# One column of a Householder step, yc, computed on VectorE behind rt instead of on GpSimd

## Chip, cores and metric

One core of a Trainium2 chip runs the whole program. Its engines are TensorE (PE, with its weight loads as PEld), VectorE (DVE), ScalarE (ACT), GpSimd (POOL) and SyncE (SP, which issues the DMAs). The metric is the device time of one execution in microseconds (us); durations of single instructions are given in ns or us.

## What is computed

The reference is a chain of four residual blocks on x of shape 128 x 64 x 128: a spectral graph layer, a mixture of eight experts, a graph layer with LSTM windows, and a second mixture of experts. Only the first block matters here, since it needs the eigenvectors of a 64 x 64 matrix:

```python
deg = jnp.sum(A, axis=0) + jnp.sum(A, axis=1) - jnp.diagonal(A)
d_inv_sqrt = jnp.where(deg > 0, jax.lax.rsqrt(deg), 0.0)
L = jnp.diag(deg) - A
L_norm = d_inv_sqrt[:, None] * L * d_inv_sqrt[None, :]
_, U = jnp.linalg.eigh(L_norm)
agg = jnp.einsum('mn,bnd->bmd', U.T, features)
h = jax.nn.relu(agg @ W1 + b1)
out = h @ W2 + b2
return jnp.einsum('nm,bmd->bnd', U, out)
```

The kernel finds U itself: it brings the matrix to tridiagonal form with 62 Householder steps, finds eigenvalues by counting sign changes, and the vectors by recurrences. The change lies in the Householder steps.

## The kernel before

The function `spectrum` writes one instruction stream for each engine (the blocks `@block.gpsimd`, `@block.scalar`, `@block.tensor`, `@block.vector`). There is no scheduler: each engine runs its stream in the order written, and the streams meet only at semaphores (`then_inc` and `wait_ge`). The 62 steps are unrolled; in step i the active columns are i+1 to 63, so the tiles shrink from 63 columns to 2. The matrix M (64 x 128) holds in its left half what is left to be reduced, and in its right half the accumulated reflections.

What one step does, with the names and lines that matter:

- The row x (on all 128 partitions, so that every lane has the whole row) has just been written by VectorE (L536). ScalarE takes its squared length s2 (L291) and the root nrm (L293). VectorE makes rnrm (L523), t (L526) and rt = 1/t (L527), the factor that normalizes the Householder vector.
- GpSimd takes the sign nsg of the leading element (L227), scales the column form xc of the row to xsc (L230) and the row to xs (L231). When rt is there it makes the column yc = xsc * rt - e (L234), then CB (L235), which keeps the off-diagonal element for later, and, when ntau is there, ntyc = yc * ntau (L238).
- TensorE makes two products with M in each step: with xsc (L384, into bank 1), which waits for M of the step before and for xsc, and with yc (L386, into bank 2). Each is a 4-byte product and shows as two matrix multiplications.
- VectorE makes the row form y of the vector (L530) behind rt, and ntau (L532). ScalarE makes q from the first product (L297) and ny = y * ntau (L299). VectorE takes the dot product h2 of y and q (L115, two instructions), and with ny, h2 and q it writes the next row x (L536).
- VectorE then updates M twice. The first update (L540) needs the second product and ntyc. Between the two stand the dot product that takes xc out of the new row (L115 with h_junk_x and h_xc) and the dot product mc. The second update (L546) writes the M that the next step's first product waits for.

So yc has two forms of use: as the weights of the second product, and as an input of ntyc. Both meet again in the first update of M, L540.

Of the kernel before, what the change touches and what calls it, by code (L numbers as in the profile page):

```python
# [8 lines left out]
ALU = mybir.AluOpType  # L9
# [5 lines left out]
N = 64  # L15
# [97 lines left out]
def dot(dve, junk, a, b, out):  # L113

    return dve.tensor_tensor_reduce(out=junk, in0=a, in1=b, scale=1.0, scalar=0.0, op0=ALU.mult, op1=ALU.add,  # L115
                                    accum_out=out)


def spectrum(nc, k, sem, A, loads, x_tok):
# [5 lines left out]
    with ExitStack() as own:  # L125
        def sb(name, shape, dtype=F32):
            return own.enter_context(nc.sbuf_tensor("h_" + name, shape, dtype))

        def col(name, rows=P):
            return sb(name, [rows, 1])[:, :]  # L130
        pivot, minus = sb("pivot", [P, P]), sb("minus", [P, N])
# [6 lines left out]
        s2, nrm, rnrm, t, rt, sg, nsg, ntau, xc, h2, nudge = (  # L138
            col(n) for n in "s2 nrm rnrm t rt sg nsg ntau xc h2 nudge".split())
        scratch = sb("scratch", [P, 2 * GT, D])  # L140
        xsc, yc, ntyc, mc = (col(n, N) for n in "xsc yc ntyc mc".split())
# [41 lines left out]
        @block.sync  # L183
        def _(sp):
            for h in range(2):
                sp.dma_start(A[:, h * N:(h + 1) * N], loads["adj"]).then_inc(s_adj, 16)
            for q in range(4):
                r = slice(q * TILES // 4, (q + 1) * TILES // 4)
                sp.dma_start(k.X[:, r, :], x_tok[:, r, :]).then_inc(s_x[q], 16)
            for dst, src in loads["rows"](rows, rows2):  # L190
                sp.dma_start(dst, src).then_inc(s_rows, 16)
            for dst, src in loads["raw"](raw):
                sp.dma_start(dst, src).then_inc(s_raw, 16)
            sp.wait_ge(s_const, CONSTS)
            for dst, src in loads["rest"]:
                sp.dma_start(dst, src).then_inc(s_load, 16)
            sp.wait_ge(s_load, 16 * len(loads["rest"]))

        @block.gpsimd
        def _(pool):  # L200
            pool.memset(ident[:, :], 0.0).then_inc(s_pool, 1)
            pool.memset(pivot[:, :], 0.0).then_inc(s_pool, 1)
            pool.wait_ge(s_pool, 2)
            pool.affine_select(out=ident[:, :], in_=ident[:, :], compare_op=ALU.not_equal, fill=1.0, base=0,
                               pattern=[[-1, P]], channel_multiplier=1).then_inc(s_pool, 1)
            consts = [pool.memset(ones[:, :], 1.0), pool.memset(BDU[:, :], 0.0), pool.memset(BDUT[:, :], 0.0), pool.memset(BDAT[:, :], 0.0),
                      pool.memset(k.upper[:, :], -1.0), pool.memset(k.w_gate1[:, :, :], 0.0)]
            consts += [pool.memset(k.prio[:, e:e + 1], float(E - e)) for e in range(E)]
            consts += [pool.iota(dst, pattern=[pattern], base=base, channel_multiplier=lanes,
                                 allow_small_or_imprecise_dtypes=True) for dst, pattern, lanes, base in  # L210
                       ((order, [0, 1], 1, 0), (k.irow[:, :], [1, IROW], 0, 0), (k.token[:, :], [P, TILES], 1, 1))]
            for ins in consts:
                ins.then_inc(s_const, 1)
            pool.memset(pivot[:, N:N + 1], 1.0).then_inc(s_const, 1)

            pool.wait_ge(s_const, CONSTS - 1)
            pool.affine_select(out=k.upper[:, :], in_=k.upper[:, :], compare_op=ALU.is_ge, fill=0.0, base=0,
                               pattern=[[-1, P]], channel_multiplier=1).then_inc(s_const, 1)
            for i in range(STEPS):
                if i == ROWS_AT:  # L220
                    pool.wait_ge(s_rows, 16 * 5)
                    pool.tensor_tensor(rows[0:SKIPS * GATES, :], rows[0:SKIPS * GATES, :], rows2[:, :],
                                       ALU.add).then_inc(s_sum, 1)
                pool.wait_ge(s_row, i + 1)
                if i:
                    pool.wait_ge(s_beta, i)
                pool.tensor_scalar(nsg, x[:, i + 1:i + 2], 0.0, -0.5, ALU.is_lt, ALU.add).then_inc(s_sign, 1)  # L227
                pool.wait_ge(s_sign, i + 1)
                pool.wait_ge(s_xcol, i + 1)
                pool.tensor_scalar(xsc, xc[0:N, :], nsg[0:N, :], 4.0, ALU.mult, ALU.mult).then_inc(s_xs, 1)  # L230
                pool.tensor_scalar(xs[:, i + 1:N], x[:, i + 1:N], nsg, 4.0, ALU.mult, ALU.mult).then_inc(s_xs, 1)  # L231
                pool.wait_ge(s_inverse, 2 * i + 1)
                pool.wait_ge(s_xs, 2 * i + 1)
                pool.tensor_scalar(yc, xsc, rt[0:N, :], minus[0:N, i + 1:i + 2], ALU.mult, ALU.add).then_inc(s_ycol, 1)  # L234
                pool.tensor_scalar(CB[:, i:i + 1], t, nsg, None, ALU.mult).then_inc(s_beta, 1)  # L235
                pool.wait_ge(s_ycol, i + 1)
                pool.wait_ge(s_inverse, 2 * i + 2)
                pool.tensor_scalar(ntyc, yc, ntau[0:N, :], None, ALU.mult).then_inc(s_ntyc, 1)  # L238

            def normalized(g, tiles):  # L240
                if g >= 2:
                    pool.wait_ge(s_tokens, g - 1)
                for j in range(tiles):
                    n = g * GT + j
                    last = pool.tensor_scalar(k.ZB[g % 2][:, j * P:(j + 1) * P], k.X[:, n, :], k.mean[:, n:n + 1],
                                              k.rstd[:, n:n + 1], ALU.subtract, ALU.mult)
                last.then_inc(s_z, 1)

            for turn in range(PASSES):
                for c in range(len(LEAVES) - 1):  # L250
                    if turn and c < len(LEAVES) - 2:
                        if turn == 1 and c == 0:
                            pool.wait_ge(s_scale, 2)
                        normalized((turn - 1) * (len(LEAVES) - 2) + c, GT)
            pool.wait_ge(s_scale, 4)
            for g in range(EARLY, GROUPS):
                normalized(g, GT // 2)
# [214 lines left out]
        def _(dve):  # L472
            link = Chain(dve, ch)
            tt_, ts_, stt = dve.tensor_tensor, dve.tensor_scalar, dve.scalar_tensor_tensor
# [43 lines left out]
            def reflect(i):  # L518

                r, rest, at = slice(i + 1, N), slice(i + 2, N), slice(i + 1, i + 2)  # L520

                dve.wait_ge(s_rooted, i + 2)
                link(dve.reciprocal(rnrm, nrm))  # L523
                if i:
                    dve.wait_ge(s_beta, i)
                link(stt(out=t, in0=rnrm, scalar=s2, in1=nrm, op0=ALU.mult, op1=ALU.add))  # L526
                dve.reciprocal(rt, t).then_inc(s_inverse, 1)  # L527
                dve.wait_ge(s_inverse, 2 * i + 1)
                dve.wait_ge(s_xs, 2 * i + 2)
                link(stt(out=y[:, r], in0=xs[:, r], scalar=rt, in1=pivot[:, N:2 * N - 1 - i],  # L530
                         op0=ALU.mult, op1=ALU.subtract))
                dve.reciprocal(ntau, y[:, at]).then_inc(s_inverse, 1)  # L532
                dve.wait_ge(s_q, i + 1)
                link(dot(dve, junk_h[:, r], y[:, r], q[:, r], h2))
                dve.wait_ge(s_scaled, i + 1)
                stt(out=x[:, rest], in0=ny[:, rest], scalar=h2, in1=q[:, rest],  # L536
                    op0=ALU.mult, op1=ALU.add).then_inc(s_row, 1)
                dve.wait_ge(s_ym, i + 1)
                dve.wait_ge(s_ntyc, i + 1)
                got_M = link.put(stt(out=M[:, i + 1:P], in0=ps[2][0:N, i + 1:P], scalar=ntyc, in1=M[:, i + 1:P],  # L540
                                     op0=ALU.mult, op1=ALU.add))
                dve.wait_ge(s_row, i + 2)
                dot(dve, junk_x[:, rest], x[:, rest], ident[:, rest], xc).then_inc(s_xcol, 1)
                link.need(got_M)
                link(dot(dve, junk_m[0:N, r], M[:, r], y[0:N, r], mc))
                stt(out=M[:, r], in0=ny[0:N, r], scalar=mc, in1=M[:, r], op0=ALU.mult, op1=ALU.add).then_inc(s_matrix, 1)  # L546

            for i in range(STEPS):
                reflect(i)
# [1945 lines left out]
```

## Time and profile before

| what | value |
|---|---|
| median of 3 runs | 1427.07 us (1426.35 to 1429.05) |
| profiled execution, its time | 1429.24 us |
| profiled execution, its span from the first to the last instruction | 1427.5 us |
| granted TensorE clock over the span | 0.902 of full speed |
| PE, PEld busy | 1110.5 us (78%), 823.2 us (58%) |
| DVE, ACT, POOL busy | 813.1 us (57%), 747.9 us (52%), 537.7 us (38%) |

The page of the profile cuts the span into 40 slices. The Householder steps fill the first four and most of the fifth, about 11 to 173 us. The shares of the whole span say little of them: there each step is a chain over four engines, and what counts is which instruction starts late in it and why. That is read from the timeline of single steps, where each row gives start, duration, engine, line and what the engine had waited for.

### The profile page before, as it was taken

The page shows a single profiled execution, that of the slowest core. Times are in us where ns is not written, and L with a number is a line of the kernel's source. Part 1 is how long each engine was busy: PE and PEld are TensorE (multiplying, and loading weights), DVE is VectorE, ACT ScalarE, POOL GpSimd, SP SyncE. Part 2 cuts the span into 40 slices and gives each one's busy share as a digit, 9 for nine tenths or more (in the row PEclk, how much of TensorE's full clock was granted, in tenths as well). Part 3 has the DMA queues.
Part 4 walks back from the last instruction along what each step waited for, and adds up shares of the span by engine and source line. Part 5 has one row for each costly group of instructions (what it writes and reads, how often), then busy time and mean ns, then how long its engine had stood idle before and what let it go on. Part 6 is the DMA issues. An engine that isn't in the chain of part 4 may idle for free. (4 is left out here: it accounts for less than half of the span.)

```text
span 1427.5 us, 27849 instructions
## 1 busy us (share of the span) xinstructions
PE 1110.5 (78%) x6302; PEld 823.2 (58%) x6303; DVE 813.1 (57%) x3799; ACT 747.9 (52%) x2079; POOL 537.7 (38%) x837
## 2 busy tenths in 40 slices
PE   3444424568744999999949999999999689929995
PEld 2223313456644999999936663445444245529995
DVE  7777798958772433354558973444444478622221
ACT  4555555515322666666626765655555366415552
POOL 5666513302577770255447500000000005645554
PEclk9999965879757999999969999999999799959998
DMA  9500000000112332333311100000000002243330
GB/s 260 144 1 1 1 1 1 1 4 16 36 64 85 118 120 66 89 103 104 102 46 50 40 1 0 0 1 0 0 1 0 4 6 85 90 130 110 106 103 27
DMA packets 85701, 75.57 MB, mean 53 GB/s; under 512 B 13207, under 2 KB 74848, under 8 KB 85613
## 3 DMA queue, kind: packets, MB, share of 16 engines
q1 hardware_dynamic: 71788, 44.64, 11.3%
q0 software_dynamic: 13824, 29.98, 6.7%
q8 instruction: 28, 0.46, 0.1%
q14 instruction: 61, 0.49, 0.1%
HBM read 41.72 MB, written 33.37 MB: 53 GB/s over the span
## 5 line engine op out<-in xcount | busy, mean ns | idle before, releaser
L1249 POOL DMA_INDIRECT z<-spent,seats x64 | 63.3, 990 | 393.5 <-DVE spent L1370 376.1
L1716 ACT ACTIVATE c_H<-ps,c_b 128x128 f32<-128x128 f32 x576 | 156.9, 383 | 99.5 <-PE ps L1762 99.5
L2278 PE MATMUL ps<-BIG,spent 128*128 x364 | 156.1, 578 | 3.3 <-ACTq L2291 3.3
L1762 PE MATMUL ps<-ZS,c_w 128*128 128x128 f32 x1152 | 142.5, 277 | 2.9 <-ACT ZS L1705 1.7
L1748 PE MATMUL ps<-spent,c_H 128*128 x1152 | 140.3, 275 | 0.0
L1762 PEld LDWEIGHTS ps<-ZS,c_w 128*128 128x128 f32 x1152 | 136.0, 194 | 3.9 <-ACT ZS L1705 2.4
L1748 PEld LDWEIGHTS ps<-spent,c_H 128*128 128x128 f32 x1152 | 134.3, 192 | 0.0
L2278 PEld LDWEIGHTS ps<-BIG,spent 128*128 128x128 f32 x364 | 69.7, 192 | 84.7 <-issue 84.7
L2286 PE MATMUL ps<-e_hs,spent 128*128 128x512 f32 (+1 forms) x256 | 110.0, 572 | 0.0
L897 POOL DMA_INDIRECT z<-BIG,spots x64 | 63.5, 993 | 111.1 <-DVE spots L1014 93.7
L1616 POOL DMA_INDIRECT c_rows<-y,seats x64 | 60.6, 946 | 113.9 <-DMA y<-c_ys 60.0
L1861 POOL DMA_INDIRECT out_dram<-X,BIG x72 | 70.5, 979 | 78.5 <-DVE X L1878 65.5
L1642 DVE COPY c_w<-spent 128x512 f32 x144 | 56.2, 433 | 75.1 <-PE ps L1762 71.0
L1897 ACT ACTIVATE j_H<-ps,bias_cols 128x256 f32<-128x256 f32 x144 | 60.4, 471 | 64.5 <-PE ps L1934 63.7
L384 PE MATMUL ps<-h_M,h_xsc 64*128 64x63 f32 (+61 forms) x124 | 37.5, 392 | 70.7 <-POOL h_xsc L230 68.5
L1661 DVE TENSOR_TENSOR c_ys<-ps,b_dn 128x128 f32<-128x128 f32 x144 | 35.2, 286 | 98.3 <-PE ps L1748 97.4
L1874 DVE TENSOR_TENSOR X<-ps,b_dn 128x128 f32<-128x128 f32 x72 | 17.6, 286 | 120.0 <-PE ps L1922 120.0
L384 PEld LDWEIGHTS ps<-h_M,h_xsc 64*128 64x128 f32 x124 | 31.0, 309 | 87.3 <-DVE h_M L546 85.9
L2286 PEld LDWEIGHTS ps<-e_hs,spent 128*128 128x128 f32 x256 | 48.6, 190 | 56.1 <-issue 53.2
L2005 POOL DMA_INDIRECT d_Y<-y,seats x64 | 63.5, 993 | 40.7 <-SPq L1989 19.4
L1621 POOL DMA_INDIRECT z<-BIG,spots x64 | 64.3, 1005 | 19.5 <-issue 19.5
L1934 PE MATMUL ps<-ZS,w_up 128*128 128x256 f32 x288 | 69.7, 386 | 1.5 <-ACT ZS L1886 1.5
(534 smaller groups left out, 2599.2 us busy)
## 6 DMA issues: line engine op xcount, KB each, us to landing
BIG<-z SPq DMA_DIRECT2D x72, 129.0 KB, 2.1
ZB<-z SPq DMA_DIRECT2D x144, 64.0 KB
y<-c_ys SPq DMA_DIRECT2D x72, 128.0 KB
spent<-in_L_ffn_W_dram SPq DMA_DIRECT2D x1, 2048.0 KB
spent<-in_L_ffn_W_dram SPq DMA_DIRECT2D x8, 256.0 KB
w_dn<-in_L_ffn_Wd_dram SPq DMA_DIRECT2D x8, 256.0 KB
z<-BIG,spots POOLq DMA_INDIRECT x128, 2.2
z<-j_padding SPq DMA_DIRECT2D x9, 129.0 KB, 2.6
```

What stands on the lines that cost most here:

```text
L384: pe.matmul(ps[1][:, r], xsc.to_broadcast([N, P]), M[:, r], start=True, stop=True).then_inc(s_xm, 1)
L897: pool.indirect_dma_start(z, bass.IndirectOffsetOnAxis(ap=k.spots[:, n, 0:1], axis=0), z_of(n), None, bounds_check=E * STRIDE - 1, oob_is_ ...
L1249: pool.indirect_dma_start(z, bass.IndirectOffsetOnAxis(ap=k.seats[:, 0, n:n + 1], axis=0), k.R[:, row(n), :], None, bounds_check=E * STRID ...
L1621: pool.indirect_dma_start(z, bass.IndirectOffsetOnAxis(ap=k.spots[:, n, 1:2], axis=0), k.BIG[:, n * P:(n + 1) * P], None, bounds_check=2 * ...
L1716: act.activation(H[u][:, c, h * P:(h + 1) * P], UP[u][c // 2][:, o:o + P], ACT.Gelu, bias=b1[u][h][:, c:c + 1]).then_inc(gelu, 1)
L1748: last = pe.matmul(Y[u][:, h * D:(h + 1) * D], H[u][:, c, h * P:(h + 1) * P], w2[:, ds(es[h] * (C * D) + c * D, D)], start=(c == 0), stop= ...
L1762: pe.matmul(UP[u][c // 2][:, o:o + P], w1[u][h][:, c * P:(c + 1) * P], ZT[u][:, h * P:(h + 1) * P], start=True, stop=True).then_inc(up, 1)
L1861: pool.indirect_dma_start(out, bass.IndirectOffsetOnAxis(ap=Z[b][h][:, ROW - 1:ROW].bitcast(I32), axis=0), ys[b][h][:, :], None, bounds_ch ...
L1934: pe.matmul(UP[u][c // 2][:, c % 2 * SLOT_TILE:(c % 2 + 1) * SLOT_TILE], k.w_up1[:, c * P:(c + 1) * P], ZT[u][:, :], start=True, stop=True ...
L2005: pool.indirect_dma_start(Y[b][:, :], None, y, bass.IndirectOffsetOnAxis(ap=k.seat[1][:, n:n + 1], axis=0)).then_inc(fetched[b], 16)
L2278: last = pe.matmul(view(k.ps[4 * u + j], wide, lanes), k.w_ihT[:, w, :], state(i, u, s, p, wide, lanes), start=True, stop=(s == 0))
L2286: pe.matmul(view(k.ps[4 * u + j], wide, lanes), k.w_hhT[:, w, :], view(hs[u], wide, lanes), start=False, stop=True).then_inc(fed, 1)
```

## The change

In each of the 62 steps the instruction that makes yc leaves the stream of GpSimd and enters that of VectorE, between rt and y. Its wait for xsc goes with it. In steps after the first VectorE also waits for the ntyc of the step before, which still reads the old yc. GpSimd's next instruction, CB, keeps the wait for rt; ntyc waits for yc by a semaphore as before.

```diff
                 pool.wait_ge(s_inverse, 2 * i + 1)
-                pool.wait_ge(s_xs, 2 * i + 1)
-                pool.tensor_scalar(yc, xsc, rt[0:N, :], minus[0:N, i + 1:i + 2], ALU.mult, ALU.add).then_inc(s_ycol, 1)
                 pool.tensor_scalar(CB[:, i:i + 1], t, nsg, None, ALU.mult).then_inc(s_beta, 1)
                 pool.wait_ge(s_ycol, i + 1)
...
                 dve.reciprocal(rt, t).then_inc(s_inverse, 1)
                 dve.wait_ge(s_inverse, 2 * i + 1)
+                dve.wait_ge(s_xs, 2 * i + 1)
+                if i:
+                    dve.wait_ge(s_ntyc, i)
+                ts_(yc, xsc, rt[0:N, :], minus[0:N, i + 1:i + 2], ALU.mult, ALU.add).then_inc(s_ycol, 1)
                 dve.wait_ge(s_xs, 2 * i + 2)
                 link(stt(out=y[:, r], in0=xs[:, r], scalar=rt, in1=pivot[:, N:2 * N - 1 - i],
```

VectorE in one step before, from t to the dot product h2 (lines as in the kernel before):

```order
L526 SCALAR_TENSOR_TENSOR h_t<-h_rnrm,h_s,h_nrm 128x1 [waits h_beta,ch]
L527 RECIPROCAL h_rt<-h_t 128x1 [waits ch]
L530 SCALAR_TENSOR_TENSOR h_y<-h_xs,h_rt,h_pivot 128x62 [waits h_xs,h_inverse]
L532 RECIPROCAL h_ntau<-h_y 128x1 [waits ch]
L115 ISA h_junk_h,h_h<-h_y,h_q 128x62 [waits h_q]
```

The same place after the change, where the line numbers below the edit are larger by two:

```order
L524 SCALAR_TENSOR_TENSOR h_t<-h_rnrm,h_s,h_nrm 128x1 [waits h_beta,ch]
L525 RECIPROCAL h_rt<-h_t 128x1 [waits ch]
L530 TENSOR_SCALAR h_yc<-h_xsc,h_rt,h_minus 64x1 [waits h_ntyc,h_xs,h_inverse]
L532 SCALAR_TENSOR_TENSOR h_y<-h_xs,h_rt,h_pivot 128x62 [waits h_xs]
L534 RECIPROCAL h_ntau<-h_y 128x1 [waits ch]
L115 ISA h_junk_h,h_h<-h_y,h_q 128x62 [waits h_q]
```

One instruction more stands between rt and y, and so ahead of ntau and everything behind it; the wait for rt (h_inverse) is now yc's.

GpSimd in one step before:

```order
L227 TENSOR_SCALAR h_nsg<-h_x 128x1 [waits h_beta,h_row]
L230 TENSOR_SCALAR h_xsc<-h_xc,h_nsg 64x1 [waits h_xcol,h_sign]
L231 TENSOR_SCALAR h_xs<-h_x,h_nsg 128x62
L234 TENSOR_SCALAR h_yc<-h_xsc,h_rt,h_minus 64x1 [waits h_xs,h_inverse]
L235 TENSOR_SCALAR h_CB<-h_t,h_nsg 128x1
L238 TENSOR_SCALAR h_ntyc<-h_yc,h_ntau 64x1 [waits h_inverse,h_ycol]
```

GpSimd in the same step after:

```order
L227 TENSOR_SCALAR h_nsg<-h_x 128x1 [waits h_beta,h_row]
L230 TENSOR_SCALAR h_xsc<-h_xc,h_nsg 64x1 [waits h_xcol,h_sign]
L231 TENSOR_SCALAR h_xs<-h_x,h_nsg 128x62
L233 TENSOR_SCALAR h_CB<-h_t,h_nsg 128x1 [waits h_inverse]
L236 TENSOR_SCALAR h_ntyc<-h_yc,h_ntau 64x1 [waits h_inverse,h_ycol]
```

CB moves up to the place of yc, and ntyc stands right behind it, with the same two waits as before.

## Rows read from the trace of the kernel before

**Rows 1.** Windows, all Householder steps: stretch, length, then busy time by engine.

```profile
11.00:173.60 162.60, 73.45 (x248) 48.56 (x248) 127.69 (x872) 90.10 (x434) 109.99 (x373) 1.00 0.28 77
```

**Rows 2.** Timeline, a step of 35 columns: start, duration, engine, line, operands, [idle before].

```profile
88.04 0.26 DVE L536 SCALAR_TENSOR_TENSOR h_x<-h_ny,h_h,h_q 128x35 f32<-128x35 f32 x1
...
88.80 0.29 POOL L230 TENSOR_SCALAR h_xsc<-h_xc,h_nsg 64x1 f32<-64x1 f32 x1 [0.18 <-DVE h_xc L115]
...
89.23 0.61 PE L384 MATMUL ps<-h_M,h_xsc 64*128 64x35 f32 x2 [1.12 <-POOL h_xsc L230]
89.40 0.17 DVE L527 RECIPROCAL h_rt<-h_t 128x1 f32<-128x1 f32 x1
89.60 0.25 DVE L530 SCALAR_TENSOR_TENSOR h_y<-h_xs,h_rt,h_pivot 128x35 f32<-128x35 f32 x1
89.67 0.40 POOL L234 TENSOR_SCALAR h_yc<-h_xsc,h_rt,h_minus 64x1 f32<-64x1 f32 x1 [0.19 <-DVE h_rt L527]
89.89 0.16 DVE L532 RECIPROCAL h_ntau<-h_y 128x1 f32<-128x1 f32 x1
89.94 0.38 ACT L297 ACTIVATE h_q<-ps,h_nudge,h_rt 128x35 f32<-128x35 f32 x1 [0.76 <-PE ps L384]
...
90.12 0.59 PE L386 MATMUL ps<-h_M,h_yc 64*64 64x99 f32 x2 [0.28 <-POOL h_yc L234]
90.22 0.31 ACT L299 ACTIVATE h_ny<-h_y,h_ntau 128x35 f32<-128x35 f32 x1
...
90.35 0.20 DVE L115 CUSTOM_DVE_ANT_0 h_junk_h<-h_y,h_q 128x35 f32<-128x35 f32 x1 [0.30 <-ACT h_q L297]
...
90.63 0.25 DVE L536 SCALAR_TENSOR_TENSOR h_x<-h_ny,h_h,h_q 128x34 f32<-128x34 f32 x1
90.80 0.31 DVE L540 SCALAR_TENSOR_TENSOR h_M<-ps,h_ntyc,h_M 64x99 f32<-64x99 f32 x1
```

**Rows 3.** Timeline, a step of 12 columns that started late on VectorE.

```profile
147.99 0.16 DVE L532 RECIPROCAL h_ntau<-h_y 128x1 f32<-128x1 f32 x1
...
148.19 0.30 ACT L299 ACTIVATE h_ny<-h_y,h_ntau 128x12 f32<-128x12 f32 x1
...
148.59 0.23 DVE L536 SCALAR_TENSOR_TENSOR h_x<-h_ny,h_h,h_q 128x11 f32<-128x11 f32 x1 [0.22 <-ACT h_ny L299]
```

**Rows 4.** Timeline, an early step of 53 columns: ntau and ny.

```profile
40.84 0.16 DVE L532 RECIPROCAL h_ntau<-h_y 128x1 f32<-128x1 f32 x1
...
41.20 0.33 ACT L299 ACTIVATE h_ny<-h_y,h_ntau 128x53 f32<-128x53 f32 x1
```

**Rows 5.** Timeline, a late step of 3 columns.

```profile
169.70 0.16 DVE L532 RECIPROCAL h_ntau<-h_y 128x1 f32<-128x1 f32 x1
...
169.98 0.28 ACT L299 ACTIVATE h_ny<-h_y,h_ntau 128x3 f32<-128x3 f32 x1
...
170.13 0.30 POOL L238 TENSOR_SCALAR h_ntyc<-h_yc,h_ntau 64x1 f32<-64x1 f32 x1
...
170.36 0.22 DVE L536 SCALAR_TENSOR_TENSOR h_x<-h_ny,h_h,h_q 128x2 f32<-128x2 f32 x1
170.53 0.28 DVE L540 SCALAR_TENSOR_TENSOR h_M<-ps,h_ntyc,h_M 64x67 f32<-64x67 f32 x1
```

**Rows 6.** Timeline, VectorE behind the steps: two scalars from memory, then one.

```profile
177.72 0.31 DVE L572 TENSOR_SCALAR h_trial<-irow,h_nwidth,h_nlo 128x64 f32<-128x64 f32 x1
178.07 0.25 DVE L573 TENSOR_SCALAR BIG<-h_trial,h_diag 128x64 f32<-128x64 f32 x1
```

**Rows 7.** Timeline, VectorE: four equal instructions in a row, and two small ones.

```profile
1132.15 1.11 DVE L1315 TENSOR_SCALAR spent<-spent,mean,rstd 128x128 f32<-128x128 f32 x4
1133.18 0.68 DVE L1271 TENSOR_TENSOR spent<-X,ps 128x512 f32<-128x512 f32 x1
...
166.25 0.22 DVE L546 SCALAR_TENSOR_TENSOR h_M<-h_ny,h_mc,h_M 64x5 f32<-64x5 f32 x1
...
166.40 0.16 DVE L523 RECIPROCAL h_rnrm<-h_nrm 128x1 f32<-128x1 f32 x1
```

## The prediction

> **What bounds the kernel now.** I read the windows first, to see how long the Householder steps last: about 162 us, in which VectorE, the busiest engine, is busy 128 us, 79%, so no engine is full and the steps are a chain [rows 1]. 62 steps in 162 us are 2.6 us each. VectorE works on without a pause behind the steps (the next stage begins from the finished M), so a step that is longer by some time moves the end by that time.
>
> Then I read one step's timeline, from one x to the next, to see which instruction starts late and on whose account [rows 2]. x starts at 88.04 and again at 90.63: 2.59 us. In between lies this cycle. x lets the first update of M start, behind it xc, then xsc on GpSimd (88.80 to 89.09), then the first product (89.23 to 89.84), then q on ScalarE (89.94), ny behind it (90.22 to 90.53), and x again at 90.63. The reader is to see two things there. First, yc on GpSimd (89.67 to 90.07) and the second product (90.12 to 90.71) are not in that cycle: they go to the first update of M at 90.80, which starts 0.17 us behind x on the same engine. Second, there is a side branch on VectorE: rt ends at 89.57, y ends at 89.85, ntau at 90.05, and ny needs ntau. It starts at 90.22, since ScalarE is busy with q. So ntau has slack, but not much.
>
> How much is told by a step in which VectorE ran late [rows 3]. There ntau ended at 148.15 and ny started at 148.19: 0.04 us is the least that lies between them. ny ended at 148.49 and x started at 148.59; the row itself puts x's 0.22 us of idle time down to ny. The same 0.10 us lies between the end of ny and x in the undisturbed steps (90.53 to 90.63 [rows 2], 170.26 to 170.36 [rows 5]). So I read x as released by ny in every step, and every delay of ny as a delay of x.
>
> **The slack of ntau.** It is the gap from the end of ntau to the start of ny, less 0.04 us. With 53 columns: 41.00 to 41.20, slack 0.16 [rows 4]. With 35: 90.05 to 90.22, slack 0.13 [rows 2]. With 3: 169.86 to 169.98, slack 0.08 [rows 5]. It shrinks because y, q and ny shrink by different amounts. I take these three for the first 20, the next 20 and the last 22 steps.
>
> **The change part by part.**
>
> *yc enters VectorE ahead of y.* y then starts later by the start-to-start distance of yc and y, which I call the shift. The trace has no VectorE instruction of one column with two scalars read from memory (rt and the column of minus), so it is bounded by rows. Four instructions of that kind with 128 columns plus the start of the next take 1133.18 - 1132.15 = 1.03 us, 0.257 each [rows 7]; that is an upper end, since yc has one column. A lower end is a small instruction with one such scalar: the second update of M with 5 columns starts at 166.25, and the next instruction at 166.40, 0.15 us later although it lasts 0.22 [rows 7]. Between the two stand two estimates. With 64 columns, an instruction with two scalars takes 0.31 us where one with a single scalar takes 0.25 [rows 6]; the second scalar costs 0.06, which added to 0.15 gives 0.21. And 127 columns taken off the 0.257 at 0.7 ns each (x is 0.03 us longer with 34 columns than with 2, about 1 ns each [rows 2, 5], and here one tensor less is read) leave 0.17. I take 0.19, their middle. The duration of yc itself comes to 0.22 + 0.06 = 0.28 us.
>
> The Trainium skill (VectorE: DVE Perf Modes, The TRN2 errata) prices a VectorE instruction from and to SBUF at 58 cycles plus its columns, which for one column at its 0.96 GHz is an estimate of 0.06 us; by that the shift would lie under the slack of every step and the sum would be nothing. The trace doesn't agree: 0.15 us is the distance behind an instruction of 5 columns [rows 7].
>
> *What the shift costs.* ny starts later by shift less slack. First 20 steps: 0.19 - 0.16 = 0.03, 0.6 us. Next 20: 0.06, 1.2 us. Last 22: 0.11, 2.4 us. Sum +4.2 us. The dot product of y and q is not delayed: it had 0.30 us of idle time in which it waited for q [rows 2], more than the shift. The new waits cost nothing: xsc ended at 89.09, before rt had started [rows 2], and the ntyc of the step before had to be there for that step's update of M.
>
> *yc leaves GpSimd.* 62 times 0.40 us of busy time [rows 2], none of it in the cycle. CB takes its place and is early, and nobody waits for it. ntyc was held by the two instructions ahead of it and now by ntau: in the late step it started at 170.13, 0.27 us behind the end of ntau [rows 5]. Now it may start about 0.1 us behind an ntau that ends 0.19 later, so about where it stood (rt to yc shows 0.10 as the time from VectorE to GpSimd [rows 2]). nsg and xsc, which are in the cycle, start after an idle wait and not behind yc.
>
> *The second product starts earlier*, by about 0.2 us: yc ends some 0.04 + 0.28 = 0.32 us behind rt and no longer 0.50 (89.57 to 90.07 [rows 2]). [...] What waits for it is the first update of M, which starts 0.17 us behind x, 0.08 before x ends [rows 2]. That is how VectorE lets instructions follow that don't wait (0.07 before the end in [rows 7]): no gain in most steps. In the late steps ntyc ends at 170.43 and the update starts at 170.53, 0.10 later [rows 5]; there the update may be held by 0.02 to 0.03 us. In those steps ntau, ny and x make the longer way, so the gain would be hidden by it.
>
> The profiled execution took 1429.24 us, so it would take 1433.4. It lies 2.2 us above the median of the runs; the forecast for the median is 1427.1 + 4.2 = 1431.3 us.
>
> **The rivals.**
>
> *The cover holds.* If yc is as cheap as the lower end (shift 0.15), the sum is 0 + 0.02 x 20 + 0.07 x 22 = 1.9 us: 1429.0; at 0.08 or less it is nothing, 1427.1. For it: the shift isn't in the trace, and at 0.17 us the sum is 0.2 + 0.8 + 2.0 = 3.0, at the edge of what can be told. Against it: the second scalar has a price in the rows [rows 6]. Chance 0.30.
>
> *Faster: the first update of M waits in every step.* If its 0.10 us behind the end of the second product (90.71 to 90.80 [rows 2]) is not slack but the time that this wait takes, an earlier product lets it follow x after 0.14 us or less and not 0.17; M, xc and xsc come earlier by 0.03 to 0.05, 62 times: -1.9 to -3.1 us, 1424.0 at best. This decides only where the shift stays below the slack, 0.08 us in the late steps, since otherwise ny holds x. For it: the 0.10 us is the same as from ny to x. Against: the distance of 0.17 us behind x is an ordinary one. Chance 0.10.
>
> *y is held until yc has finished.* The shift is the whole duration of yc and the 0.04 us from an end to the next start, 0.32, and the sum 0.16 x 20 + 0.19 x 20 + 0.24 x 22 = 12.3 us: 1439.4. The Trainium skill (VectorE: DVE Perf Modes, The DRAIN you can't avoid) says that the next operation doesn't start until the pipe has emptied. The rows show the opposite for instructions that don't need each other: x lasts from 90.63 to 90.88 and the update starts at 90.80 [rows 2], and yc and y are such a pair. Chance 0.06.
>
> **How the numbers follow.** The forecast, shift 0.19, has 0.54. It is 1431.3 us; its own bounds are the shift of 0.17 (+3.0, 1430.1) and of 0.257 (0.10 x 20 + 0.13 x 20 + 0.18 x 22 = 8.4 us, 1435.5). The range of 8 in 10 takes in the rival with the cover down to no loss and half a microsecond for what the runs differ by, 1426.5, and ends at 1435.5; the faster rival and the held y are left out, 0.16 together. A measurement of this kernel can tell about 0.2%, 2.9 us, from no change. Slower by more: the forecast and the held y, 0.60. Within: the cover, 0.30. Faster: 0.10.
>
> **What would show it.** Right: yc on VectorE lasts 0.25 to 0.30 us, and y starts about 0.19 behind it; from the end of ntau to ny is 0.04 us in nearly all steps, and ny starts 0.30 to 0.38 us behind q and no longer 0.26 to 0.30; x's idle time is put down to ny in nearly all steps; the late steps last 2.50 us and the early ones hardly longer than now; the stretch of the steps grows by about 4 us and the rest of the span doesn't. Wrong: gaps from ntau to ny of more than 0.05 us (the cover held), or an update of M that follows x closer than 0.15 us while the steps get shorter (it had waited for the product), or a distance from yc to y as long as yc itself. Steps that start late for a reason the profile doesn't name, as that of [rows 3], may fall elsewhere in another program; I price that at nothing and leave it to the range.

## The result, and the profile after

The changed kernel takes 1431.61 us (median of 18 runs, 1427.55 to 1433.28) where the kernel before takes 1427.15 us (18 runs, 1425.09 to 1429.29): a ratio of 1.0025 with a 95% interval of 1.0018 to 1.0032. It is slower by about 4 us, as forecast (1431.3). The profiled execution has a span of 1431.1 us.

The stretch of the Householder steps, in the windows view of the kernel after (columns as in [rows 1]; it now ends at 177):

```profile
11.00:177.00 166.00, 73.33 (x248) 48.50 (x248) 137.50 (x932) 93.71 (x434) 89.66 (x311) 1.00 0.27 76
```

VectorE has gained about 10 us of busy time (this window ends 0.5 us before the last step does, so it counts 60 more instructions and not 62), GpSimd has lost 62 instructions and 20 us, and the stretch is longer. The last update of M in the timeline shows by how much, first in the kernel before, then in the kernel after:

```profile
173.43 0.21 DVE L546 SCALAR_TENSOR_TENSOR h_M<-h_ny,h_mc,h_M 64x2 f32<-64x2 f32 x1
...
177.31 0.21 DVE L548 SCALAR_TENSOR_TENSOR h_M<-h_ny,h_mc,h_M 64x2 f32<-64x2 f32 x1
```

It ended at 173.64 and now ends at 177.52. From there to the end of the span it was 1253.9 us and is 1253.6 us now. The whole difference lies in the steps.

The step of 35 columns, the one of [rows 2], in the timeline of the kernel after (lines below the edit are two larger on VectorE and two smaller on GpSimd, TensorE and ScalarE):

```profile
89.11 0.26 DVE L538 SCALAR_TENSOR_TENSOR h_x<-h_ny,h_h,h_q 128x35 f32<-128x35 f32 x1
...
90.30 0.61 PE L382 MATMUL ps<-h_M,h_xsc 64*128 64x35 f32 x2 [1.37 <-POOL h_xsc L230]
90.47 0.16 DVE L525 RECIPROCAL h_rt<-h_t 128x1 f32<-128x1 f32 x1
90.67 0.27 DVE L530 TENSOR_SCALAR h_yc<-h_xsc,h_rt,h_minus 64x1 f32<-64x1 f32 x1
...
90.86 0.24 DVE L532 SCALAR_TENSOR_TENSOR h_y<-h_xs,h_rt,h_pivot 128x35 f32<-128x35 f32 x1
...
90.99 0.59 PE L384 MATMUL ps<-h_M,h_yc 64*64 64x99 f32 x2
91.01 0.38 ACT L295 ACTIVATE h_q<-ps,h_nudge,h_rt 128x35 f32<-128x35 f32 x1 [0.76 <-PE ps L382]
91.13 0.16 DVE L534 RECIPROCAL h_ntau<-h_y 128x1 f32<-128x1 f32 x1
91.33 0.32 ACT L297 ACTIVATE h_ny<-h_y,h_ntau 128x35 f32<-128x35 f32 x1
...
91.46 0.31 POOL L236 TENSOR_SCALAR h_ntyc<-h_yc,h_ntau 64x1 f32<-64x1 f32 x1 [0.43 <-DVE h_ntau L534]
...
91.75 0.25 DVE L538 SCALAR_TENSOR_TENSOR h_x<-h_ny,h_h,h_q 128x34 f32<-128x34 f32 x1
91.92 0.30 DVE L542 SCALAR_TENSOR_TENSOR h_M<-ps,h_ntyc,h_M 64x99 f32<-64x99 f32 x1
```

The reader is to see four distances. yc lasts 0.27 us and y starts 0.19 behind it. ntau ends at 91.29 and ny starts at 91.33: 0.04 us, where 0.17 lay before. ny starts 0.32 us behind q, no longer 0.28. ny ends at 91.65 and x starts at 91.75, 0.10 us as before. The step lasts 2.64 us and lasted 2.59. The update of M follows x after 0.17 us, as before, although its product is now done at 91.58, 0.34 us ahead of it, where it was done only 0.09 ahead (90.71 to 90.80).

A late step, the one of 3 columns [rows 5]:

```profile
173.39 0.16 DVE L534 RECIPROCAL h_ntau<-h_y 128x1 f32<-128x1 f32 x1
173.59 0.30 ACT L297 ACTIVATE h_ny<-h_y,h_ntau 128x3 f32<-128x3 f32 x1
...
173.99 0.22 DVE L538 SCALAR_TENSOR_TENSOR h_x<-h_ny,h_h,h_q 128x2 f32<-128x2 f32 x1 [0.21 <-ACT h_ny L297]
```

Here x stands idle for 0.21 us and the row puts it down to ny; before, the same x had no idle time in its row. The view of waits lists this 22 times, 20 of them in the last 22 steps, and gives VectorE's wait for q as almost gone (2.2 us, where it was 18.0):

```profile
DVE h_x L538 <- ACT h_ny L297: 4.2, 22, 0.4
...
DVE h_junk_h L115 <- ACT h_q L295: 2.2, 9, 0.5
```

### The profile page after: what moved, and what is told of

The parts are those of the page before. It is cut to its first block and busy times, and to the rows that moved or that the text cites. A ratio compares the mean times of both kernels' runs of the same rounds, so it can differ in the third digit from the quotient of the medians.

```text
span 1431.1 us, 27787 instructions
## 1 busy us (share of the span) xinstructions
PE 1109.8 (78%) x6302; PEld 822.6 (57%) x6303; DVE 824.0 (58%) x3861; ACT 750.5 (52%) x2079; POOL 518.5 (36%) x775
## 3 DMA queue, kind: packets, MB, share of 16 engines
q1 hardware_dynamic: 71788, 44.64, 11.2%
```

## The experiments

Two theories were set against each other first. The slack theory is that of the prediction: one instruction ahead of y moves ntau by 0.19 us, and ny and x follow by what exceeds the slack. Its rivals: the loss comes with taking yc from GpSimd or with the earlier product, or VectorE is simply too full.

The table has every run: the time, its ratio to the kernel before on the same chip (which took 1427.39, 1427.67 and 1427.27 us in the three series of experiments), and from the profile the length of the steps (from the first rnrm to the end of the last update of M) and the median from one x to the next in the first 20, the next 20 and the last 22 steps. The rest of the span differs from execution to execution by several us (1249.6 to 1255.3 among these profiles), so the length of the steps is the sharper of the two.

| kernel | time, us | ratio, 95% interval | steps, us | from x to x, us |
|---|---|---|---|---|
| before | 1427.15 | | 161.85 | 2.765, 2.595, 2.450 |
| after | 1431.61 | 1.0025 (1.0018 to 1.0032) | 165.64 | 2.785, 2.635, 2.530 |
| copy ahead of y | 1431.57 | 1.0026 (1.0016 to 1.0037) | 165.61 | 2.780, 2.635, 2.550 |
| copy behind ntau | 1427.13 | 0.9998 (0.9990 to 1.0007) | 161.67 | 2.760, 2.585, 2.440 |
| yc with one scalar | 1429.78 | 1.0012 (1.0003 to 1.0021) | 162.94 | 2.760, 2.580, 2.480 |
| double shift | 1442.17 | 1.0102 (1.0087 to 1.0117) | 176.30 | 2.955, 2.820, 2.720 |
| yc on ScalarE | 1424.11 | 0.9973 (0.9962 to 0.9984) | 158.83 | 2.700, 2.535, 2.425 |
| yc behind ntau | 1433.47 | 1.0042 (1.0028 to 1.0056) | 167.60 | 2.860, 2.670, 2.525 |
| ny on VectorE | 1424.91 | 0.9983 (0.9974 to 0.9992) | 159.43 | 2.715, 2.575, 2.440 |
| ny on VectorE, yc on ScalarE | 1420.87 | 0.9953 (0.9939 to 0.9967) | 156.38 | 2.660, 2.520, 2.390 |
| q's waits swapped | 1425.00 | 0.9983 (0.9974 to 0.9993) | 158.55 | 2.700, 2.545, 2.400 |
| x's waits swapped | 1429.17 | 1.0008 (0.9997 to 1.0020) | 163.42 | 2.790, 2.630, 2.465 |
| four swaps | 1427.35 | 1.0007 (0.9997 to 1.0016) | 162.29 | 2.750, 2.620, 2.470 |
| yc on ScalarE, three swaps | 1425.71 | 0.9990 (0.9980 to 1.0000) | 160.59 | 2.710, 2.575, 2.450 |

### One more instruction ahead of y

```diff
                 dve.wait_ge(s_inverse, 2 * i + 1)
+                dve.wait_ge(s_xs, 2 * i + 1)
+                link.put(ts_(spare, xsc, rt[0:N, :], minus[0:N, i + 1:i + 2], ALU.mult, ALU.add))
                 dve.wait_ge(s_xs, 2 * i + 2)
```

> The kernel before, with yc still on GpSimd, and one more VectorE instruction between rt and y in each step: the same two-scalar operation as yc, written to a spare column that nobody reads. Slack theory (y and ntau shift by 0.19 us, ny and x follow by what exceeds the slack): as the changed kernel, +3.5 to +4.5 us, gap from ntau to ny 0.04 us in all steps, late steps about 2.50 us. Rival A (the loss comes with taking yc from GpSimd, or with the earlier second product): no loss, within 0.5 us of before. Rival B (VectorE is simply fuller, every added instruction costs its own 0.19 us): 62 x 0.19 = 11.8 us.

The timeline of its step of 35 columns:

```profile
90.20 0.27 DVE L530 TENSOR_SCALAR h_spare<-h_xsc,h_rt,h_minus 64x1 f32<-64x1 f32 x1
90.27 0.41 POOL L234 TENSOR_SCALAR h_yc<-h_xsc,h_rt,h_minus 64x1 f32<-64x1 f32 x1 [0.18 <-DVE h_rt L527]
90.39 0.24 DVE L532 SCALAR_TENSOR_TENSOR h_y<-h_xs,h_rt,h_pivot 128x35 f32<-128x35 f32 x1
...
90.66 0.16 DVE L534 RECIPROCAL h_ntau<-h_y 128x1 f32<-128x1 f32 x1
90.73 0.59 PE L386 MATMUL ps<-h_M,h_yc 64*64 64x99 f32 x2 [0.30 <-POOL h_yc L234]
90.86 0.32 ACT L299 ACTIVATE h_ny<-h_y,h_ntau 128x35 f32<-128x35 f32 x1
```

yc is where it was, on GpSimd, and the second product still waits for it; only the spare instruction stands ahead of y, and the gap from ntau (90.82) to ny is 0.04 us. The steps take 165.61 us, against 165.64 for the changed kernel. So the whole loss comes with the place on VectorE, none of it with GpSimd or the product, and it is a third of the 11.8 us that a full engine would cost.

### The same instruction behind ntau

```diff
                 dve.reciprocal(ntau, y[:, at]).then_inc(s_inverse, 1)
+                link.put(ts_(spare, xsc, rt[0:N, :], minus[0:N, i + 1:i + 2], ALU.mult, ALU.add))
```

> The same spare instruction, yc still on GpSimd, but behind ntau, where VectorE waits 0.25 to 0.30 us for q. Slack theory: y and ntau stand where they stood, the dot product still waits for q, no loss (within 0.7 us of before), steps of 2.60 us in the middle and 2.39 us at the end. Rival B (VectorE is fuller, or the longer instruction stream costs): the same loss as with the spare instruction ahead of y, 4 to 12 us.

```profile
89.54 0.16 DVE L532 RECIPROCAL h_ntau<-h_y 128x1 f32<-128x1 f32 x1
89.59 0.38 ACT L297 ACTIVATE h_q<-ps,h_nudge,h_rt 128x35 f32<-128x35 f32 x1 [0.76 <-PE ps L384]
89.62 0.25 DVE L533 TENSOR_SCALAR h_spare<-h_xsc,h_rt,h_minus 64x1 f32<-64x1 f32 x1
...
89.87 0.31 ACT L299 ACTIVATE h_ny<-h_y,h_ntau 128x35 f32<-128x35 f32 x1
```

The timeline has the spare instruction while q is still at work; ny stands 0.28 us behind q and 0.17 behind ntau, as in [rows 2]. The time is that of before, 0.9998. The same 62 instructions cost 3.8 us at one place and nothing at the other.

### The size of the shift

yc in a form with one scalar and two tensors, and the changed kernel with a spare copy of yc behind yc:

```diff
-                ts_(yc, xsc, rt[0:N, :], minus[0:N, i + 1:i + 2], ALU.mult, ALU.add).then_inc(s_ycol, 1)
+                stt(out=yc, in0=xsc, scalar=rt[0:N, :], in1=minus[0:N, i + 1:i + 2], op0=ALU.mult, op1=ALU.add).then_inc(s_ycol, 1)
```

> The changed kernel, with yc written as an operation with one scalar and two tensors of one column in place of two scalars. Slack theory: duration 0.22 us and shift 0.14 to 0.15 us in place of 0.27 and 0.19, so +0.5 to +2 us against before and 2 to 3 us less than the changed kernel; late steps about 2.45 us. If the loss comes with yc leaving GpSimd or with the earlier product: as the changed kernel, +4 us.

```diff
                 ts_(yc, xsc, rt[0:N, :], minus[0:N, i + 1:i + 2], ALU.mult, ALU.add).then_inc(s_ycol, 1)
+                link.put(ts_(spare, xsc, rt[0:N, :], minus[0:N, i + 1:i + 2], ALU.mult, ALU.add))
```

> The changed kernel with a second, spare copy of the yc instruction behind yc. Slack theory: the shift is 0.38 us, so 0.22 x 20 + 0.25 x 20 + 0.30 x 22 = 16 us against before, about 12 us against the changed kernel: all of the second 0.19 us is paid, since no slack is left. A theory of a fixed loss (yc leaving GpSimd): still +4 us. A loss in proportion to the shift: twice 4, +8 us.

The first, then the second, each from its timeline:

```profile
89.64 0.21 DVE L530 SCALAR_TENSOR_TENSOR h_yc<-h_xsc,h_rt,h_minus 64x1 f32<-64x1 f32 x1
89.78 0.24 DVE L532 SCALAR_TENSOR_TENSOR h_y<-h_xs,h_rt,h_pivot 128x35 f32<-128x35 f32 x1
...
90.05 0.16 DVE L534 RECIPROCAL h_ntau<-h_y 128x1 f32<-128x1 f32 x1
90.26 0.31 ACT L297 ACTIVATE h_ny<-h_y,h_ntau 128x35 f32<-128x35 f32 x1
```

```profile
95.13 0.26 DVE L530 TENSOR_SCALAR h_yc<-h_xsc,h_rt,h_minus 64x1 f32<-64x1 f32 x1
95.32 0.26 DVE L531 TENSOR_SCALAR h_spare<-h_xsc,h_rt,h_minus 64x1 f32<-64x1 f32 x1
...
95.50 0.24 DVE L533 SCALAR_TENSOR_TENSOR h_y<-h_xs,h_rt,h_pivot 128x35 f32<-128x35 f32 x1
...
96.40 0.25 DVE L539 SCALAR_TENSOR_TENSOR h_x<-h_ny,h_h,h_q 128x34 f32<-128x34 f32 x1 [0.31 <-ACT h_ny L297]
```

With one scalar yc lasts 0.21 us and y follows after 0.14. In this step ny still stands 0.05 us behind ntau, so the slack just holds; the early and middle steps are no longer than before, the late ones by 0.03 us, and the steps by 1.1 us. With the second copy y stands 0.37 us behind yc, and the steps take 14.5 us more than before, 10.7 more than with one copy: 62 x 0.18 = 11.2 if all of the second one is paid. The loss is thus no fixed price of the move and not in proportion to the shift. It is what the shift exceeds the slack by: about 1, 4 and 14.5 us for 0.14, 0.19 and 0.37.

### yc on ScalarE

On VectorE the lines that make yc, with their waits, are left out of the changed kernel; ScalarE gets them ahead of q:

```diff
                 act.wait_ge(s_inverse, 2 * i + 1)
+                act.wait_ge(s_xs, 2 * i + 1)
+                if i:
+                    act.wait_ge(s_ntyc, i)
+                act.activation(yc, xsc, ACT.Identity, bias=minus[0:N, i + 1:i + 2], scale=rt[0:N, :]).then_inc(s_ycol, 1)
                 act.wait_ge(s_xm, i + 2)
```

> yc neither on GpSimd nor on VectorE: ScalarE makes it right behind rt, in the 0.33 to 0.41 us in which it waits for the first product. y and ntau stay where they are in the kernel before; the second product starts 0.1 to 0.2 us earlier. Slack theory: no loss, and at most 0.5 us of gain in the late steps, where ntyc held the first update of M: 1426.5 to 1427.5 against a before of 1427.1. Rival (the update of M waits for the second product in every step, the faster rival of the prediction): 1.9 to 3.1 us faster. A loss would show that yc on ScalarE delays q.

The steps became 3.0 us shorter and the time 3.9 us (by the ratio), as much as the rival had claimed and not the 0.5 us of the slack theory. The timeline, from the first product to the update of M:

```profile
87.17 0.61 PE L386 MATMUL ps<-h_M,h_xsc 64*128 64x35 f32 x2 [1.14 <-POOL h_xsc L230]
...
87.53 0.39 ACT L297 ACTIVATE h_yc<-h_xsc,h_minus,h_rt 64x1 f32<-64x1 f32 x1 [0.42 <-DVE h_rt L529]
...
87.83 0.37 ACT L299 ACTIVATE h_q<-ps,h_nudge,h_rt 128x35 f32<-128x35 f32 x1
87.97 0.59 PE L388 MATMUL ps<-h_M,h_yc 64*64 64x99 f32 x2 [0.20 <-ACT h_yc L297]
...
88.51 0.25 DVE L538 SCALAR_TENSOR_TENSOR h_x<-h_ny,h_h,h_q 128x34 f32<-128x34 f32 x1
88.68 0.30 DVE L542 SCALAR_TENSOR_TENSOR h_M<-ps,h_ntyc,h_M 64x99 f32<-64x99 f32 x1
```

The second product ends at 88.56, early enough, and yet the update follows x after the same 0.17 us. So the rival's mechanism isn't at work. What moved is q: it starts at 87.83, 0.05 us behind the end of the first product (87.78); in [rows 2] it started 0.10 behind it (89.84 to 89.94). (In the medians of the thirds it is 0.04, 0.05 and 0.11: in the late steps q starts at a fixed 0.33 us behind rt, with yc ahead of it on ScalarE, and the product is no longer what it waits for.) q used to wait for rt and then for the product; here yc waits for rt, and q has only the product to wait for. Why that brings q forward was tried further down.

### yc on VectorE, behind ntau

From its place ahead of y in the changed kernel yc goes down behind ntau:

```diff
                 dve.reciprocal(ntau, y[:, at]).then_inc(s_inverse, 1)
+                if i:
+                    dve.wait_ge(s_ntyc, i)
+                ts_(yc, xsc, rt[0:N, :], minus[0:N, i + 1:i + 2], ALU.mult, ALU.add).then_inc(s_ycol, 1)
```

> yc on VectorE, but behind ntau in the idle time before the dot product, where the spare copy cost nothing. Slack theory: ny and x are not delayed, but yc ends 0.63 to 0.68 us behind rt and no longer 0.50, and the second product with it: it ends 1.41 us (early), 1.31 (middle), 1.17 (late) behind rt, and the first update of M, 0.04 later, at 1.45, 1.35, 1.21 where it stood at 1.32, 1.23, 1.12. So 0.13 x 20 + 0.12 x 20 + 0.09 x 22 = 7 us slower than before, the gap from ntau to ny as before, and the update's idle time put down to the product. If the place behind ntau were free, as the spare copy was: no loss.

```profile
92.80 0.25 DVE L533 TENSOR_SCALAR h_yc<-h_xsc,h_rt,h_minus 64x1 f32<-64x1 f32 x1
...
93.11 0.59 PE L384 MATMUL ps<-h_M,h_yc 64*64 64x99 f32 x2 [0.43 <-DVE h_yc L533]
...
93.47 0.26 DVE L537 SCALAR_TENSOR_TENSOR h_x<-h_ny,h_h,h_q 128x34 f32<-128x34 f32 x1
93.73 0.31 DVE L541 SCALAR_TENSOR_TENSOR h_M<-ps,h_ntyc,h_M 64x99 f32<-64x99 f32 x1
```

The product ends at 93.70 and the update starts 0.03 us behind it, 0.26 behind x and not 0.17. The steps take 5.8 us more (7 expected). So yc had only a little slack on GpSimd: a yc that ends about 0.15 us later holds M, and a yc that ends earlier than GpSimd's gains nothing.

### ny on VectorE, alone and with yc on ScalarE

```diff
-                act.wait_ge(s_inverse, 2 * i + 2)
-                act.activation(ny[:, r], y[:, r], ACT.Copy, scale=ntau).then_inc(s_scaled, 1)
...
                 dve.reciprocal(ntau, y[:, at]).then_inc(s_inverse, 1)
+                dve.wait_ge(s_inverse, 2 * i + 2)
+                link.put(ts_(ny[:, r], y[:, r], ntau, None, ALU.mult))
                 dve.wait_ge(s_q, i + 1)
                 link(dot(dve, junk_h[:, r], y[:, r], q[:, r], h2))
-                dve.wait_ge(s_scaled, i + 1)
```

> The kernel before, with ny made by VectorE behind ntau (in its idle time before the dot product) and no longer by ScalarE behind q. If x is released by ny, 0.10 us behind its end, x is now released by h2, which ended 0.07 to 0.08 us ahead of x and lets it start 0.04 behind: 0.03 to 0.04 us less in each of the first 40 steps, less in the late ones, where the update of M is held by ntyc: 1.0 to 1.5 us faster. If x was released by h2 already: no change. If ny on VectorE delays the dot product: slower.

> ny on VectorE and yc on ScalarE together: x is released by h2 in all steps, and neither ntyc nor the second product holds the update of M. 0.03 to 0.04 us in each of 62 steps, 1.9 to 2.5 us faster than before (ratio about 0.9985). If only one of the two works: as that one alone.

The first alone took 2.4 us off the steps, where 1.0 to 1.5 were expected: 0.05, 0.02 and 0.01 us per step in the medians, 1.6 in all, and the rest in single steps that no longer started late. The timeline of the two together:

```profile
87.14 0.24 DVE L534 TENSOR_SCALAR h_ny<-h_y,h_ntau 128x35 f32<-128x35 f32 x1
...
87.51 0.08 DVE L115 DVE_READ_ACCUMULATOR2_ANT h_h<- 128x1 f32 x1
87.62 0.25 DVE L537 SCALAR_TENSOR_TENSOR h_x<-h_ny,h_h,h_q 128x34 f32<-128x34 f32 x1
```

ny now ends 0.24 us ahead of x, and x starts 0.03 us behind h2, the only thing it still waits for. With ny early, x comes earlier. By itself this doesn't show that ny had released x, the step on which the prediction rested: the edit also takes away one of x's two waits, and in the kernel before h2 ended later than ny, 0.08 us ahead of x. Its row in the step of [rows 2]:

```profile
90.47 0.08 DVE L115 DVE_READ_ACCUMULATOR2_ANT h_h<- 128x1 f32 x1
```

The distances over all steps of the kernel before settle it. From the end of ny to x it is 0.10 us in 61 of the 62 steps; from the end of h2 to x it is anything from 0.05 to 0.22 us in the same steps. In the kernel with q's waits swapped (further down) the distance from h2 goes from 0.035 to 0.24 us in as many steps, and that from ny is again 0.10 in 61 steps.

Together with yc on ScalarE the kernel takes 1420.87 us, 6.8 less than before (expected 1.9 to 2.5). Its steps are 5.5 us shorter, about the sum of the 2.4 of ny and the 3.0 of q's gain above; the other 1.3 us lie outside the steps, where executions differ by several us. It beats both kernels, with a ratio of 0.9953 (0.9939 to 0.9967) to the kernel before.

### The order of two waits

The gain of q was left open. Two theories: a wait that stands behind another one and ends last costs more than one that stands first or alone; or q is early because ScalarE had just been at work.

```diff
-                act.wait_ge(s_inverse, 2 * i + 1)
                 act.wait_ge(s_xm, i + 2)
+                act.wait_ge(s_inverse, 2 * i + 1)
```

> The kernel before, in which q on ScalarE waits for the first product first and for rt second, instead of rt first. Nothing else changes. With yc on ScalarE q had only the wait for the product left and started 0.05 us behind the product's end where it starts 0.10 behind it in the kernel before, and the steps were 0.06 us shorter. Theory of the second wait (a wait that stands behind another one and ends last costs some 0.06 us more than one that stands first): q starts 0.04 to 0.05 us behind the product, the early and middle steps are 0.05 to 0.06 us shorter, the late ones less, since ntyc holds the update of M there: 2 to 3 us faster. Theory of the busy engine (q is early only because ScalarE had just been at work on yc): no change.

```profile
87.20 0.61 PE L384 MATMUL ps<-h_M,h_xsc 64*128 64x35 f32 x2 [1.06 <-POOL h_xsc L230]
...
87.84 0.38 ACT L297 ACTIVATE h_q<-ps,h_nudge,h_rt 128x35 f32<-128x35 f32 x1 [0.70 <-PE ps L384]
```

q starts 0.03 us behind the product, and nothing but the order of the two waits has changed; ScalarE was idle before it. The steps are 3.3 us shorter (the late ones too, by 0.05 us, which I hadn't expected), as with yc on ScalarE. The order of the waits is the cause; the earlier product isn't.

At x the swap puts ny first and h2 second:

> The kernel before, in which x on VectorE waits for ny first and for h2 second, instead of h2 first. Theory of the second wait: x starts 0.04 us behind the end of ny and no longer 0.10, the early and middle steps are 0.04 to 0.06 us shorter, the late ones hardly: 1.5 to 3 us faster. If 0.10 us is what any wait of VectorE for ScalarE's ny takes: no change.

```profile
91.09 0.31 ACT L299 ACTIVATE h_ny<-h_y,h_ntau 128x35 f32<-128x35 f32 x1
...
91.36 0.08 DVE L115 DVE_READ_ACCUMULATOR2_ANT h_h<- 128x1 f32 x1
91.54 0.25 DVE L537 SCALAR_TENSOR_TENSOR h_x<-h_ny,h_h,h_q 128x34 f32<-128x34 f32 x1
```

No gain: the steps take 1.6 us more. Now x starts 0.10 us behind h2 (91.44) and 0.14 behind ny (91.40). The two end within 0.04 us of each other, so whichever wait stands second sets x, at 0.10. The expectation had overlooked that. A swap gained where the other wait had long been met (q), and not where both end together (x).

> The kernel before with the order of two waits swapped at four places: q (product first), x (ny first), xsc (the column xc first, the sign second), first update of M (ntyc first, second product second). yc stays on GpSimd. Theory of the second wait: 0.05 to 0.06 us less at each of q, x and xsc, until ntau (slack 0.15, 0.13, 0.09 us, and x itself 0.06 earlier behind ny) or the second product holds the step: 0.10 to 0.17 us per step, 6 to 10 us faster. If the single swaps show nothing: no change.

> yc on ScalarE (q then has a single wait) with the swaps at x, xsc and the first update of M. Theory of the second wait: the gain of yc on ScalarE, 3.9 us, and 0.05 to 0.10 us per step more until ntau holds ny: 7 to 10 us faster than before, and no worse than the four swaps alone where the second product holds the update of M there.

Both fell short: 6 to 10 and 7 to 10 us were expected, and the steps take 0.4 us more and 1.3 us less than before. With the four swaps xsc does start 0.10 us behind xc (0.17 before), but then ntau holds ny (0.03 to 0.04 us between them in 59 of the 62 steps), and the second product holds the update of M, now as its second wait:

```profile
90.10 0.59 PE L386 MATMUL ps<-h_M,h_yc 64*64 64x99 f32 x2 [0.39 <-POOL h_yc L234]
...
90.47 0.25 DVE L537 SCALAR_TENSOR_TENSOR h_x<-h_ny,h_h,h_q 128x34 f32<-128x34 f32 x1
90.79 0.31 DVE L541 SCALAR_TENSOR_TENSOR h_M<-ps,h_ntyc,h_M 64x99 f32<-64x99 f32 x1
```

The product ends at 90.69, the update starts 0.10 us later and 0.32 behind x. With yc on ScalarE the product is in time, but x is 0.13 us behind ny, and q can't come before yc is through. These two changed several places at once; how much each swap gives alone, beside q's and x's, stays open.

## Why the prediction was right

- **The bound.** x is released by ny, 0.10 us behind its end. It held in the kernel before in 61 of 62 steps and in the kernel after (0.10 in the median of each third of the steps). What I didn't know is that 0.10 us goes with a wait that stands second: behind h2 x needs the same 0.10 when h2's wait stands second and 0.04 when it is the only one.
- **The shift.** 0.19 us was taken from the middle of the estimates; it measured 0.19 us in the median of each third, and yc lasts 0.27 (0.28 worked out). y did not wait for yc to finish: yc ran from 90.67 to 90.94, and y started at 90.86, so the rival of the held y fell. The forecast gave only half of what the Trainium skill (VectorE: DVE Perf Modes, The DRAIN you can't avoid) says: right behind the sentence on the pipe that must empty it adds that a next operation that is not held starts earlier. This pair agrees with the addition, by 0.08 us. The 0.06 us that the forecast worked out from the table of the Trainium skill (VectorE: DVE Perf Modes, The TRN2 errata) is a third of the 0.19 us from yc to y; that section says itself that this row of the table gives too little for a single operation.
- **The slack.** In 59 of the 62 steps ntau and ny are now at most 0.05 us apart; in the kernel before 3 were. The cover was gone in nearly every step, as the forecast said.
- **The sum.** Forecast were +0.6, +1.2 and +2.4 us for the three stretches of steps, 4.2 in all. Measured from x to x they are +0.95, +0.6 and +2.1, 3.6 in all, and 3.8 over the whole stretch. By medians the steps grew by 0.02, 0.04 and 0.08 us where 0.03, 0.06 and 0.11 were forecast, which makes 3.0 us. The other 0.6 us are the balance of single steps that last up to 0.35 us longer than their neighbours, partly other ones than before; the forecast priced them at nothing, no run explains them, and that they bring the sum closer to 4.2 is luck. The term that was too large is the growth of each step, the late one most. For one thing y is about 0.02 us shorter in the kernel after (0.21 for 0.23 in the late steps), which gives part of the shift back. In the kernel with the spare copy late y keeps its 0.23 us, and the late steps grow by 0.10. What makes y shorter wasn't tried. For another, the slack of the late steps was read from the step of 3 columns, 0.08 us; in the median of the last 22 steps it is 0.09.
- **GpSimd.** ntyc starts 0.17 us behind ntau (two waits, the second ends last), not 0.1. It cost nothing: the update follows x after 0.19, 0.17 and 0.15 us, as fast as before or faster.
- **A sign that was wrong.** x's idle time was to be put down to ny in nearly all steps; the view lists it in 22. In the other steps the gap behind h2 is there (0.10 and 0.13 us in the medians of the first two thirds), but it is not listed; all idle times listed for x are of 0.15 us and more. The late steps last 2.53 us in the median, not 2.50.
- **The rivals.** With a yc of one scalar and a shift of 0.14 us the cover would in the main have held: 1.0012, within 0.2%, as the rival with a shift of 0.15 said (1.9 us forecast, 1.1 in the steps, 2.4 in time). The faster rival fell: an earlier product does not bring the update of M closer to x.

## What to carry to other kernels

An instruction moved to another engine is to be priced by what it pushes back on the new engine, less the slack of that, and not by its own time: the same 62 instructions cost 3.8 us ahead of y and nothing behind ntau. Before moving work to make a result earlier, look whether anyone is waiting for it; here nobody waited for an earlier second product. And where an instruction waits for two semaphores and one has been met well before, try the one that ends last first in the code: at q that gave 2.3 us. At x, whose two waits end within 0.04 us of each other, it gave nothing.

## What the runs showed that I had not expected

The place of a wait has a price. In medians, q on ScalarE starts 0.10 us behind the product that it waits for when that wait stands second, and 0.04 to 0.05 us when it stands first or alone. The first update of M on VectorE starts 0.04 us behind the product as its first wait and 0.11 as its second; x starts 0.10 behind the second of its waits, whichever that is, and 0.04 behind a single one. On GpSimd xsc starts 0.17 us behind xc as the second wait and 0.10 as the first (this swap was run only together with others). Swapping q's two waits, with no other edit, is worth 2.3 us of 1427 (ratio 0.9983, 0.9974 to 0.9993). How the engines handle two waits, the runs don't show.
